# Cross-attention with a whole-batch normalisation: the cross term and the low sum moved into the step that makes them, the bias rows made on the chip

## What is computed

```python
q = _conv1x1(Wq, bq, y).reshape(B, H, Dh, -1)
k = _conv1x1(Wk, bk, y).reshape(B, H, Dh, -1)
v = _conv1x1(Wv, bv, x).reshape(B, H, Dh, Lx)
scores = jnp.einsum('bhdl,bhel->bhde', q, k) / jnp.sqrt(jnp.float32(E))
attn = jax.nn.softmax(scores, axis=-1)
out = jnp.einsum('bhde,bhel->bhdl', attn, v).reshape(B, E, Lx)
o = _conv1x1(Wo, bo, out) + x
mu = jnp.mean(o, axis=(1, 2), keepdims=True)
var = jnp.var(o, axis=(1, 2), keepdims=True)
o_hat = (o - mu) * jax.lax.rsqrt(var + EPS)
return o_hat * gn_w[None, :, None] + gn_b[None, :, None]
```

## Time and profile before

| | us |
|---|---|
| median of 3 runs (186.92 to 188.99) | 187.91 |
| the profiled execution's own time | 188.77 |
| its span | 187.0 |
| busy in the span: PE / DVE / ACT / POOL | 172.1 / 150.4 / 140.3 / 114.1 |

### The profile page before, as it was taken

One profiled execution on the slowest core, in us unless ns is written; L12 is line 12 of the kernel. 1 busy time (PEld: TensorE's weight loads), 2 busy tenths in 40 slices (PEclk: granted clock), 3 DMA queues, 4 the chain that ended last, 5 costly groups with the idle time before them and its releaser, 6 DMA issues. The chain is left out here.

```text
span 187.0 us, 4165 instructions
## 1 busy us (share of the span) xinstructions
PE 172.1 (92%) x996; PEld 127.9 (68%) x996; DVE 150.4 (80%) x554; ACT 140.3 (75%) x354; POOL 114.1 (61%) x170
## 2 busy tenths in 40 slices
PE   7777999999999999999999999999999999998640
PEld 7666776767777777777776777877777777765310
DVE  1746888999998998989989999899889999975531
ACT  4425588888888888888888988888888988777032
POOL 3775577766766677767776677667676777611020
PEclk9979999999999999999999999999999999999785
DMA  6798769898988889989888987988889755522223
GB/s 210 262 417 329 254 197 306 316 288 311 330 294 302 314 282 337 341 294 324 315 301 289 319 333 300 332 297 276 324 315 317 254 209 213 204 117 112 112 112 112
DMA packets 14409, 50.83 MB, mean 272 GB/s; under 512 B 1728, under 2 KB 1856, under 8 KB 14400
## 3 DMA queue, kind: packets, MB, share of 16 engines
q1 hardware_dynamic: 13968, 50.34, 75.7%
q10 hardware_dynamic: 432, 0.40, 0.8%
HBM read 33.95 MB, written 16.78 MB: 271 GB/s over the span
## 5 line engine op out<-in xcount | busy, mean ns | idle before, releaser
L506 PE MATMUL o_ps<-x_sb,m_sb 128*128 128x512 f32 x128 | 71.5, 647 | 0.0
L506 PE MATMUL g_ps<-hl_sb 128*128 128x258 f32 x256 | 47.0, 308 | 0.6 <-DVE hl_sb L416 0.6
L416 DVE TENSOR_TENSOR hl_sb<-y_sb,hl_sb 128x512 fp32r<-128x512 f32 x64 | 44.3, 693 | 2.4 <-ACT hl_sb L325 2.4
L269 POOL TENSOR_TENSOR rstd<-veps,nhalf 128x1 f32<-128x1 f32 x32 | 27.3, 853 | 26.9 <-DVE veps L421 26.9
L297 POOL TENSOR_TENSOR lsuma<-hl_sb 128x256 f32<-128x256 f32 x32 | 23.8, 743 | 30.2 <-DVE hl_sb L416 30.2
L325 ACT CAST hl_sb<-y_sb 128x512 fp32r<-128x512 f32 x64 | 39.1, 614 | 4.0 <-DMA y_sb<-in_ctx_dram 4.0
L362 ACT ACTIVATE out_sb<-o_ps,shift,gain 128x1024 f32<-128x1024 f32 (+1 forms) x32 | 38.3, 1198 | 0.2
L506 PEld LDWEIGHTS g_ps<-hl_sb 128*128 128x128 f32 x256 | 35.6, 195 | 0.8 <-issue 0.8
L506 PEld LDWEIGHTS ps_ps<-wqT,g_sb 128*128 128x128 f32 x64 | 9.7, 191 | 24.9 <-DVE g_sb L444 19.0
L452 DVE BATCH_NORM_STATS2 bn<-o_ps 128x6 f32<-128x512 f32 x32 | 22.3, 698 | 4.9 <-PE o_ps L506 1.2
L284 POOL TENSOR_TENSOR lsum<-lsuma,lsumb 128x256 f32<-128x256 f32 x32 | 23.3, 727 | 4.3
(11 more groups left out here) (57 smaller groups left out, 309.8 us busy)
## 6 DMA issues: line engine op xcount, KB each, us to landing
y_sb<-in_ctx_dram SPq DMA_DIRECT2D x32, 512.0 KB, 4.8
x_sb<-in_x_dram SPq DMA_DIRECT2D x32, 512.0 KB, 5.0
out_dram<-out_sb SPq DMA_DIRECT2D x31, 512.0 KB, 4.2
out_dram<-out_sb SPq DMA_DIRECT2D x2, 256.0 KB, 2.2
w_in<-in_weights_dram ACTq DMA_DIRECT2D x1, 256.0 KB, 8.8
rows<-in_biases_dram ACTq DMA_DIRECT2D x1, 128.0 KB, 6.5
cols<-in_columns_dram ACTq DMA_DIRECT2D x1, 3.0 KB, 3.4
```

The costliest lines, as they stand in the source:

```text
L269: nc.gpsimd.tensor_tensor(rstd[:, h1:h1 + 1], veps[:, h1:h1 + 1], nhalf[:, :], ALU.pow).then_inc(rstd_ready, 1)
L416: nc.vector.tensor_tensor(hl_sb[:, ky, chunks, C:2 * C], y_sb[:, ky, chunks, :], hl_sb[:, ky, chunks, 0:C].bitcast(F32), ALU.subtract).the ...
L506: return nc.tensor.matmul(dst, lhsT, rhs, start=start, stop=stop, **more)
```

## The change

Four edits:

1. On PE the transposed cross term and the low sum of batch t−1 are added at the end of step t, behind its Gram products, and not in step t+1 between the two halves of x. The 8 Gram products now stand together, the two halves of x too.
2. The low sum of batch 0 alone is made by 8 small products on PE, straight from hl_sb; POOL does nothing for batch 0.
3. The rows bqB and bkB are made on the chip: DVE scales the identity by a column (diag), PE multiplies it by a constant matrix, ACT copies both rows. The load of rows is gone. The warm-up is 8 products instead of 12.
4. On DVE g_sb and s_sb move ahead of zinv and of both statistics, both statistics stand together, and p_sb comes ahead of the aggregation. The exceptions for steps 34 and 35 are changed.

```diff
-GRAM_BEFORE_M = 6
-WARM_UP = 12
+EARLY = 1
+WARM_UP = 8
...
-            act.dma_start(rows[:, :, :].rearrange("p v e -> p (v e)"),
-                          biases.rearrange("(a v) e -> a (v e)", a=1).broadcast_to([P, 2 * E])).then_inc(c_loaded, 16)
             act.dma_start(w_in[:, :, :].rearrange("p w c -> p (w c)"), weights).then_inc(w_loaded, 16)
...
+                if is_step(t, 0):
+
+                    act.wait_ge(rows_ready, 1)
+                    nc.scalar.copy(bqB[:, :], row_ps[:, 0, :]).then_inc(rows_copied, 1)
+                    nc.scalar.copy(bkB[:, :], row_ps[:, 1, :]).then_inc(rows_copied, 1)
...
+            dve.wait_ge(c_loaded, 16)
+            nc.vector.tensor_scalar(diag[:, 0, :], ident[:, 0:P], bq_raw, SCALE * E, ALU.mult, ALU.mult).then_inc(const_dve, 1)
+            nc.vector.tensor_scalar(diag[:, 1, :], ident[:, 0:P], bk_raw, -float(E), ALU.mult, ALU.mult).then_inc(const_dve, 1)
...
-                if has(t, 2):
-
-                    pe.wait_ge(b2_copied, t - 1)
-                    product(g_ps[:, 0:C], b2_sb[:, :], ident_r[:, :], start=False, skip_group_check=True)
-                    if is_step(t, 2):
-                        keep_busy(FILL)
-                    pe.wait_ge(lsum_ready, t - 1)
-                    product(g_ps[:, 2 * C:HL], lsum[:, h, :], ones_r[:, :], start=False,
-                            skip_group_check=True).then_inc(g_ready, 1)
...
+                if has(t, 4):
+                    products_of_x(1)
+                if has(t, 2):
+                    query_product()
+                if has(t, 3):
+                    softmax_product()
                 if has(t, 1):
+                    pe.wait_ge(l_ready, t * 2 - 1)
...
+                    gram_products(range(0, HCH))
                     pe.wait_ge(l_ready, t * 2)
+                    last = gram_products(range(HCH, CH))
+                    if is_step(t, EARLY):
+
+                        for c in range(CH):
+                            last = product(g_ps[:, 2 * C:HL], hl_sb[:, 0, c, C:2 * C], ones_r[:, :], start=False,
+                                           skip_group_check=True)
+                    last.then_inc(hl_ready, 1)
...
+                if has(t, 1):
+
+                    pe.wait_ge(b2_copied, t)
+                    transposed = product(g_ps[:, 0:C], b2_sb[:, :], ident_r[:, :], start=False, skip_group_check=True)
+                    if is_step(t, EARLY):
+                        transposed.then_inc(g_ready, 1)
+                    else:
+                        pe.wait_ge(lsum_ready, t - EARLY)
+                        product(g_ps[:, 2 * C:HL], lsum[:, h1, :], ones_r[:, :], start=False,
+                                skip_group_check=True).then_inc(g_ready, 1)
```

More of the change, by code:

```diff
@@ L14 @@
 UNROLL = 4
-N_CONST = 2
 LAGS = 5
-GRAM_BEFORE_M = 6
-WARM_UP = 12
+EARLY = 1
+WARM_UP = 8
 FILL = 2
@@ L421, in variance @@
                     nc.vector.tensor_scalar(veps[:, h1:h1 + 1], var_ps, -1.0, EPS, ALU.mult, ALU.add).then_inc(veps_ready, 1)
-                if has(t, 5) and not is_step(t, RUSH + 1):
+                if has(t, 5):
                     variance()
@@ L557, in mean, with gram_products @@
                     product(mu_ps, onesn[:, :], mrow[:, h:h + 1]).then_inc(mu_ready, 1)
+                def gram_products(chunks):
+                    kg = (k - 1) % UNROLL
+                    for c in chunks:
+                        mm = product(g_ps[:, 0:HL], hl_sb[:, kg, c, 0:C], hl_sb[:, kg, c, :],
+                                     start=(c == 0), stop=(c == CH - 1))
+                    return mm
                 if has(t, 5) and not is_step(t, RUSH + 1):
@@ L587, in step @@
                     query_product()
-                if has(t, 3) and not is_step(t, RUSH):
+                if has(t, 3):
                     softmax_product()
-                def gram_products(chunks):
-                    kg = (k - 1) % UNROLL
-                    for c in chunks:
-                        mm = product(g_ps[:, 0:HL], hl_sb[:, kg, c, 0:C], hl_sb[:, kg, c, :],
-                                     start=(c == 0), stop=(c == CH - 1))
-                    return mm
                 if has(t, 1):
-                    pe.wait_ge(l_ready, t * 2)
+                    pe.wait_ge(l_ready, t * 2 - 1)
                     if exists(t, 2):
                         pe.wait_ge(s_copied, t - 1)
-                    gram_products(range(0, GRAM_BEFORE_M))
+                    gram_products(range(0, HCH))
+                    pe.wait_ge(l_ready, t * 2)
+                    last = gram_products(range(HCH, CH))
[4 more added lines that the diff above has]
+                    last.then_inc(hl_ready, 1)
                 if has(t, 3):
@@ L611, in step @@
                     mean()
-                if has(t, 1):
-                    gram_products(range(GRAM_BEFORE_M, CH)).then_inc(hl_ready, 1)
-                if is_step(t, 1):
-                    keep_busy(FILL)
                 if has(t, 2):
```

96 lines of the change are left out of this document (49 added, 47 removed).

## The result

The changed kernel takes 175.79 us (median of 4 runs, 175.33 to 176.09), the kernel before 187.41 us beside it (4 runs, 186.50 to 188.99). The ratio is 0.937, with a 95% interval of 0.930 to 0.944. The forecast was 177.0 in 173.0 to 183.5. The profiled execution of the changed kernel took 175.87 us and has a span of 174.1 us, against 187.0.

A forecast was written before the change was run, and what follows sets the result against it. Two tied cycles of 5.02 us, DVE's and PE's, were taken to bound the step. 17.1 + 28 × 4.78 + 13.36 + 12.02 = 176.3 us of span, 178.1 for the profiled execution; forecast 177.0, range 173.0 to 183.5.

The forecast's parts named there:

- Steady step: Half 0 of x to the next half 0: 4.75 us, 4.78 with the loop's head, instead of 5.055.
- The loop's head: Put at 0.035 us a step, together with keep: the mean step of 5.055 above the 5.02 shown.
- two cycles tie: DVE's and PE's cycles both hold the steady step at 5.02 us; DVE's would become 4.61.
- the 0.19 that I gave to p_sb: On DVE, p_sb follows the second statistics after 0.61 us, where the aggregation came after 0.80.
- What is late next: In the changed step of 4.75 us: the mean, then dev, vrow and m_sb, above DVE's cycle of 4.61.
- Cover of the cross term: ACT's copy ends at 4.03, PE comes to the cross term at 4.20: 0.17 us to spare.
- the first rival: The wait moves to the cross term, PE waiting for ACT's copy: step 4.98, time 182.6 us; chance 0.17.
- The third rival: Slower: the cross term's copy falls a whole output pass behind; step 5.82, time 206 us; chance 0.03.
- The hole: DMA at 57 GB/s between 5 and 6 us, laid to rows; without it weights land 1.9 us earlier.
- Start behind the weights: Query product at 10.25, first score minimum 2.8 later, first x product at 17.1 us instead of 18.89.
- brings nothing by itself: First low sum on PE instead of POOL: no gain, as both end before the weights land.
- Drain and end: Steps 32 to 35 take 13.36 us instead of 14.56, 1.2 less; the 12.02 us behind them stay.

The follow-up runs named there:

- the run with the unused load: The changed kernel, which also issues the load of the bias rows ahead of that of the weights, read by nothing: 179.78 us, ratio 0.967.
- the run with the filling: The kernel before with six products that feed nothing ahead of the mean of step 34, in PE's idle time: 185.27 us, ratio 0.9985.

## Why the prediction was right, and where not

**Steady step: right, by its own steps.** Forecast 4.78 on average, measured 4.803. The points within the step came out nearly one by one: query 1.74 (1.80), mean 3.54 (3.56), copy 3.76 (3.71), PE's turn at the cross term 4.20 (4.21), next half 0 4.75 (4.73). Half 1 at 0.87 has 0.86 against it, by the statistics. The loop's head was mis-sized: 0.035 a step, where the change has 0.23 at every turn and one slow step, together 0.07. The cause of the old price I had only guessed. That the sum fits is in part luck. It goes by PE's points, with DVE's cycle at 4.61 below them; that cycle turned out at 4.73, just no longer than PE's.

**Which edit does it: not seen.** I wrote that two cycles tie and that "both must get shorter, and the change acts on both". The runs agree, but it is DVE's order that acts on both, with 0.20 by itself. Its run confirms the 0.19 that I gave to p_sb: DVE's cycle there is 4.82, against 5.02 − 0.19 = 4.83. Whether taking away the query's wait alone "would bring nothing" isn't shown, since no run moved g_sb without p_sb in the kernel before. The 0.22 that PE's moves take out ahead of half 1 arrive on DVE too (second statistics at 2.00 instead of 2.23). But 0.13 of them go into the longer subtraction, and the step at the loop's turn is no shorter than with DVE's order alone (4.96 and 4.95), so 0.05 are left in the mean. What I didn't see is that PE's moves alone lose 0.14: they take away the work that covers DVE's first statistics. And p_sb's place, worth 0.19 on DVE's cycle with PE's old order, is worth 0.06 on top of the changed kernel with its loops written out.

**What is late next: right, but one of three.** I named the mean, then dev, vrow and m_sb. The run with a product less shows this chain, and the one with a product more shows PE's queue at nearly the same length. DVE's cycle, which I put at 4.61, is the third: with the mean 0.17 earlier dev did not move, and with the subtraction 0.21 later it did. The term mis-sized is the 0.60 from the subtraction to dev, which is 0.73, and 4.61 + 0.13 = 4.74. What I had left out is POOL: the subtraction, which lay 3.66 behind half 0 (84.71 to 88.37 in the earlier trace rows) and now lies 3.23 behind it, runs into POOL's last addition and ends 0.1 late, and dev with it (+3.96, the subtraction's end at +4.03).

**Cover of the cross term: right.** 0.24 measured for 0.17, and the first rival's mechanism appears when the score products no longer stand ahead. The third rival (a whole output pass late) got no support from any run.

**The hole: right in cause, low in size.** Rows was its cause (the run with the unused load). I took 2.0 us for the weights; it was 2.8. wqT came at 7.63 against 8.7. The rule of the Trainium skill that spoke against it ("DMA: Bandwidth & Descriptors", Specifications; line rate from 512 bytes on) doesn't hold for this load: 128 KB in 1 KB per partition, all from one 1 KB source, took 6.5 to 7.0 us, with 57 to 60 GB/s in all of the DMA engines meanwhile. Whether the piece size or the shared source makes it slow wasn't tried.

**Start behind the weights.** Query at 9.38 (forecast 10.25), the minimum 2.04 after it (2.8, taken as halfway between two clock levels; it was the full one), first product 4.45 after that (4.07). Sum 15.87 against 17.1. That the first low sum on PE "brings nothing by itself" failed: it brings 1.6 us of the time and 1.5 of the span, part of it clock. I had compared POOL's end with weights that land at 8.7; they landed earlier, and POOL's sum (9.7) was then the last to come.

**Drain and end.** 13.42 for the three steps against 13.36. The end took 10.32 and not 12.02: the clock stayed up, a gain of 1.6 I had named and not counted. The 2.2 us between 176.3 and 174.1 of span are thus −1.2 from the start, +0.6 from the steady steps, +0.1 from the drain and −1.7 from the end. So the forecast came out 1.2 us too high in time (177.0 for 175.79) by errors that partly cancel, and the largest is clock, which differs between executions of the kernel before.

## What to carry over

When two orders of work are changed together, look for what each covers of the other: moving PE's small products out from between two long ones paid only because DVE had made the next product's input ahead of time, and lost without it. When an operation moves, look also at what then runs beside it on GpSimd. Take a tied step as three queues, not one, and test each with a product more and one less before moving anything. A broadcast load of a few numbers can hold back everything behind it; here it stood at the start, and leaving it out was worth 2.8 us on the weights' way.

## What the runs showed of the hardware

- Idle time of PE at either end can cost clock afterwards, and not in every execution. With the unused load PE was idle from 9.5 to 11.6 us and ran at 0.50 (1.2 GHz) from 13 to 18; without the load it stayed at 1.00. In the run with the filling, whose start is that of the kernel before, PE was busy for 0.08 of the stretch from 9 to 10 us and for 0.05 of that from 14 to 15, and the clock stayed at 1.00. The kernel before at full clock throughout (its run with the filling) has a span of 183.9 instead of 187.0, and its runs spread over 4.8 us, those of the changed kernel over 0.8. Some 3 of the 12.9 us of span are this: 1.7 at the end, about 1.3 at the start.
- A load of 128 KB that broadcasts 1 KB to 128 partitions took 7.0 us and left 60 and 102 GB/s in the two stretches from 5 to 7 us, where without it 406 and 424 moved.
- A loop turn on PE and DVE cost 0.23 us in a tied step, and 24 steps written out cost nothing that shows.
- DVE's low-part subtraction, 128 by 512, took 0.69 us by itself and up to 1.22 when it began within a sum of POOL. Over all traces the time lost is that to POOL's end less 0.14. Where the subtraction came first, a sum of 0.46 us took 1.01.
